# Cross-attention and mixture-of-experts kernel: steps at single places, fewer direct tanh pieces, token lists in 8 by 64

## What is computed

```
x = layernorm(features)                       # 4 x 1024 x 256
h = tanh(txt_proj[:, None] + feat_proj[:, :, None] + b)      # tokens x 77 x 256
rho = einsum('bftd,d->bft', h, w)             # then masked
att = softmax(rho)
w_s, b_s = tanh(att @ text @ Wcw + bcw), tanh(att @ text @ Wcb + bcb)
x = x + (w_s * layernorm(x) + b_s)
...
probs = softmax(layernorm(x) @ gate)
scores, token_idx = top_k(probs.T, k=512)     # for each of 8 experts
out_tok = gelu(tok @ W1 + b1) @ W2 + b2       # times score, added at token_idx
x = x + routed + gelu(x @ Ws1 + bs1) @ Ws2 + bs2
```

## Time and profile before

| | |
|---|---|
| three runs | median 888.53 us (888.24 to 889.59) |
| profiled execution | 887.3 us, of which span 885.5 us |
| TensorE busy | 798.3 us, 90% |
| ScalarE busy | 759.4 us, 86% |
| VectorE busy | 714.6 us, 81% |
| GpSimd busy | 304.9 us, 34% |

### The profile page before, as it was taken

How to read it: one execution, slowest core, us unless ns; L and a number is a source line. 1 busy time by engine, 2 the same in 40 slices (tenths; PEclk the granted TensorE clock), 3 DMA queues, 4 the chain that set the end, 5 groups by cost and what they waited for, 6 DMA issues and landing times.

```text
span 885.5 us, 14111 instructions
## 1 busy us (share of the span) xinstructions
PE 798.3 (90%) x5385; PEld 471.8 (53%) x5385; DVE 714.6 (81%) x1403; ACT 759.4 (86%) x589; POOL 304.9 (34%) x534
## 2 busy tenths in 40 slices
PE   6976678669997999989999899999989999999996
PEld 5321123114442444444454455555766999999886
DVE  5899889898989699997889996895886877666641
ACT  3999999999999999999999999997752676676672
POOL 3200540615443006674002650042404145555424
PEclk9898999899999999999999999999999999999999
DMA  8000000000001000200000010003102365554513
GB/s 260 28 1 0 1 1 1 1 24 1 25 1 48 1 1 25 73 1 1 24 1 1 24 49 1 24 2 119 48 24 84 115 160 143 144 110 123 138 20 41
DMA packets 32406, 41.82 MB, mean 47 GB/s; under 512 B 2365, under 2 KB 29011, under 8 KB 32339
## 3 DMA queue, kind: packets, MB, share of 16 engines
q1 hardware_dynamic: 26083, 32.49, 11.1%
q0 software_dynamic: 6144, 8.39, 5.9%
q10 hardware_dynamic: 112, 0.04, 0.0%
HBM read 28.33 MB, written 12.58 MB: 46 GB/s over the span
## 4 chain that ended last, share of the span: by engine, by line
PE 48%; ACT 24%; DVE 19%; issue 5%; POOL 2%; DMA 1%; POOLq 0%; ACTq 0%; DVEq 0%
ACT z L1001 21%; DVE z L1389 11%; PE bank L920 10%; PE bank L793 10%; PE bank L943 9%; PE bank L850 6%; PE bank L835 5%; PE bank L768 2%; ACT z L997 1%; PE bank L720 1%; DVE att L1460 1%; PE bank L958 1%; ACT u L1050 1%; PE bank L823 1%; POOL xn L1146 1%
## 5 line engine op out<-in xcount | busy, mean ns | idle before, releaser
L1001 ACT ACTIVATE z<-z 128x4096 f32<-128x4096 f32 (+5 forms) x157 | 521.3, 3361 | 7.1 <-DVE z L1389 7.0
L1389 DVE TENSOR_SCALAR z<-feat,txt_bias 128x1024 f32<-128x1024 f32 (+1 forms) x722 | 417.9, 652 | 30.2 <-PE bank L793 29.4
L793 PE MATMUL bank<-z,window 128*32 128x512 f32 x2464 | 301.4, 614 | 61.2 <-ACT z L1001 60.2
L793 PEld LDWEIGHTS bank<-z,window 128*32 128x32 f32 x2464 | 68.1, 111 | 244.3 <-issue 133.2
L850 PE MATMUL bank<-ws_sb,u 128*128 128x256 f32 x512 | 127.2, 389 | 1.4 <-ACT u L1050 1.4
L850 PEld LDWEIGHTS bank<-ws_sb,u 128*128 128x128 f32 x512 | 93.5, 191 | 36.1 <-issue 20.2
L835 PE MATMUL bank<-tr,ws_s 128*128 128x512 f32 x384 | 108.3, 418 | 2.9 <-issue 2.9
L920 PE MATMUL bank<-xg_s,w_s 128*128 128x512 f32 x384 | 99.6, 397 | 0.2 <-DVE xg_s L1712 0.2
L1207 POOL TENSOR_TENSOR scale<-wb,x_ry 128x4 f32<-128x4 f32 x7 | 9.2, 1319 | 253.6 <-ACT wb L1012 253.6
L943 PEld LDWEIGHTS bank<-w_s,hid_s 128*128 128x128 f32 x672 | 86.3, 188 | 4.0
L943 PE MATMUL bank<-w_s,hid_s 128*128 128x256 f32 x672 | 88.2, 280 | 0.0
(11 more groups left out here) (275 smaller groups left out, 777.7 us busy)
## 6 DMA issues: line engine op xcount, KB each, us to landing
w_raw<-in_L_ffn_W_dram SPq DMA_DIRECT2D x16, 1024.0 KB, 5.7
x_ring<-in_x_dram SPq DMA_DIRECT2D x8, 512.0 KB, 7.9
xn_dram<-xn SPq DMA_DIRECT2D x8, 512.0 KB, 2.9
out_dram<-x_ring SPq DMA_DIRECT2D x8, 512.0 KB, 3.2
u<-in_L_ffn_Ws_dram SPq DMA_DIRECT2D x1, 1024.0 KB, 11.8
ws_sb<-in_L_ffn_Ws_dram SPq DMA_DIRECT2D x1, 1024.0 KB, 14.5
xg<-xn_dram,idx POOLq DMA_INDIRECT x32, 4.4
out_dram<-y,idx POOLq DMA_INDIRECT x32, 3.9
```

Source lines behind the costliest of these rows:

```text
L793: ins = e.matmul(sums[v][32 * g:32 * g + 32, :], window[:, c, 31 - at_row:63 - at_row], z[:, n % ZB, at_piece:at_piece + TOK], start=(v, g ...
L1001: e.activation(part, part, ACT.Tanh).then_inc(signal(*step), 1)
L1389: ins = e.tensor_scalar(z[:, n % ZB, i * width:(i + 1) * width], feat_of(units, c), bias_of(units, t, c), None, ALU.add)
```

## The change

- Direct pieces: 64 before, 25 after. The first eight blocks have 7, 5, 0, 4, 1, 3, 1, 1 (before 4, 3, 3, 3, 2, 2, 2, 2); later only blocks 10, 109 and 124 have one (before: 15, 45, 60, 75, 90, 105, 120 and every block that belongs to one unit, 31 to 38 and 129 to 156).
- `PRE`, `TAIL`, `FFN`: places for each unit and slice instead of tables shared by several units and a start with a step.
- Lists: a place (0 to 511) is split into 8 groups of 64 instead of 4 of 128. `pick` is 40 wide (of 64) instead of 20 (of 32), `onehot` 64 instead of 128; the matmul uses two column groups of 64; `listed` writes two halves with a mask `side`.
- Other numbers of filler pieces; `ENDS_BEHIND`, `LAST_END`, `TOGETHER_FROM`.

```diff
-FIRST_DIRECT = (4, 3, 3, 3, 2, 2, 2, 2)
-DIRECT_EVERY = (15, 1)
+FIRST_DIRECT = (7, 5, 0, 4, 1, 3, 1, 1)
+DIRECT = (10, 109, 124)
...
-TAIL_EARLY = (0, 0, 1, 2, 3, 4, 4, 5, 4, 11, 6, 10, 12, 12, 14)
+TAIL = (
+    (2, 3, 4, 6, 5, 7, 8, 9, 10, 20, 10, 13, 14, 15, 22),
...
-FFN = ((8, 2.2), (34, 2.1), (13, 2.3), (36, 2.0), (13, 1.5), (26, 1.6))
+FFN = (
+    (47, 47, 51, 53, 54, 55, 58, 62),
...
-TOGETHER, TOGETHER_FROM = 2, 93
-ENDS_BEHIND = 6
+TOGETHER, TOGETHER_FROM = 2, 91
+ENDS_BEHIND = 3
...
-TAIL_FILL = (7, 3)
-TEST_FILL = (4, 4, 6, 4, 7, 3, 5, 5, 2, 3)
-RANK_FILL = (1, 3, 6, 4)
-EXPERT_FILL = (23, 4, 0)
-SECOND_FILL = (8, 3, 2, 2, 9)
-LIST_FILL = (0, 1, 0, 0)
-LAST_END = 1
+TAIL_FILL = (8, 2)
+TEST_FILL = (5, 5, 4, 5, 7, 4, 3, 6, 4, 4)
+RANK_FILL = (1, 4, 3, 4)
+EXPERT_FILL = (27, 4, 0)
+SECOND_FILL = (8, 4, 0, 2, 11)
+LIST_FILL = (2, 1, 0, 1)
+LAST_END = 0
...
-    if len(units) > 1:
-        return 1 if n % DIRECT_EVERY[0] == 0 and len(pieces) > 2 else 0
-    return 1 if n % DIRECT_EVERY[1] == 0 else 0
+    return 1 if n in DIRECT else 0
...
-                        g = tile % G
-                        ins = e.matmul(dst[32 * g:32 * g + 32, 0:P], pick[:, tile, :], onehot[:, tile, :],
-                                       start=tile < G, stop=tile >= NT - G)
+                        g = tile % 2
+                        ins = e.matmul(dst[LOW * g:LOW * (g + 1), 0:LOW], pick[:, tile, :], onehot[:, tile, :],
+                                       start=tile < 2, stop=tile >= NT - 2)
...
+                    link(e.memset(pick[:, :, V * HIGH:LOW], 0.0))
...
-                    e.tensor_copy(picked[:], banks[LIST][:, 0:P]).then_inc(signal(*step), 1)
+                    for h in range(2):
+                        ins = e.tensor_scalar(picked[:, h * LOW:(h + 1) * LOW], banks[LIST][:, 0:LOW], side[:, h:h + 1], None, ALU.mult)
+                    ins.then_inc(signal(*step), 1)
```

More of the change, by code:

```diff
@@ L161, in work_order @@
         before = starts[bb - 1]
-        at_slots(before, PRE_EARLY, pre(early))
-        at_slots(before, PRE_LATE, pre(late))
+        at_slots(before, PRE[early - 1], pre(early))
+        at_slots(before, PRE[late - 1], pre(late))
         base, early, late = starts[bb], early - UPB, late - UPB
-        at_slots(ends_at[early] + 1, TAIL_EARLY if early else TAIL_FIRST, tail(early))
-        at_slots(base, TAIL_LATE, tail(late))
+        at_slots(ends_at[early] + 1, TAIL[early], tail(early))
+        at_slots(base, TAIL[late], tail(late))
     base = ends_at[va] + 1
[L168 to L172, removed]
+    at_slots(base, TAIL[va], tail(va))
+    for v, places in enumerate(FFN):
+        for m, n in enumerate(places):
             parts = (0, J // 2, J) if v == va - 1 and m == M - 1 else (0, J)
@@ L387, in xattn_moe_kernel @@
     NL = 3
+    HIGH, LOW = 8, 64
     CANDIDATES = (1 << DIGIT) - 1
@@ L390, in xattn_moe_kernel @@
     assert D % P == 0 and CAP == TOK and I <= 32 and NT % JT == 0 and NH == 2 and UNITS % 2 == 0 and P % E == 0
+    assert HIGH * LOW == CAP and HIGH == 2 * A and 2 * LOW == P
     assert T % G == 1 and G == UPB * C and I < 32
@@ L458, in xattn_moe_kernel @@
         V = 5
-        pick = sb("pick", [P, NT, 32], BF16)
         vals = sb("vals", [P, NT, E, V], BF16)
-        iota_slot = gt[:, 0:P]
+        iota_slot = gt[:, 0:LOW]
         bits = tested[:].bitcast(I32).rearrange("p (t e) -> p t e", e=E)
@@ L499, in xattn_moe_kernel @@
         w2_raw = sb("w2_raw", [P, M, D])
-        onehot = sb("onehot", [P, NT, P], BF16)
-        in_tile = sb("in_tile", [P, NT, A], BF16)
+        onehot = sb("onehot", [P, NT, LOW], BF16)
+        pick = sb("pick", [P, NT, LOW], BF16)
+        in_tile = sb("in_tile", [P, NT, HIGH], BF16)
         found = sb("found", [P, V, A])
@@ L1157, in _ @@
             e.memset(b2_raw, 0.0).then_inc(consts, 1)
-            e.memset(pick[:], 0.0).then_inc(consts, 1)
             e.memset(mask_h[0:1], 0.0)
             e.memset(ones_h[0:1, :], 1.0).then_inc(consts, 1)
-            e.iota(iota_slot, [[1, P]], base=0, channel_multiplier=0,
+            e.iota(iota_slot, [[1, LOW]], base=0, channel_multiplier=0,
                    allow_small_or_imprecise_dtypes=True).then_inc(consts, 1)
-            e.iota(iota_a[:], [[1, A]], base=0, channel_multiplier=0,
+            e.iota(iota_a[:], [[1, HIGH]], base=0, channel_multiplier=0,
                    allow_small_or_imprecise_dtypes=True).then_inc(consts, 1)
@@ L1421, in _ @@
                     link(e.tensor_reduce(expert_of[:], ident[:].rearrange("p (t e) -> p e t", e=E), AX.X, ALU.add))
-                    e.tensor_reduce(fold[:], ident[:].rearrange("p (g r) -> p r g", r=32), AX.X, ALU.add)
+                    e.tensor_reduce(fold[:], ident[:].rearrange("p (g q h) -> p q g h", g=2, h=2), AX.XY, ALU.add)
+                    e.tensor_reduce(side[:], ident[:].rearrange("p (q h) -> p h q", h=2), AX.X, ALU.add)
                     e.wait_ge(vector_link, linked)
@@ L1661, in _ @@
                     e.wait_ge(*done("slots"))
[L1662 to L1663 removed]
+                    link(e.tensor_scalar(eq[:].bitcast(I32), slot_i[:], LOW - 1, None, ALU.bitwise_and))
+                    link(e.tensor_scalar(gt[:].bitcast(I32), slot_i[:], LOW.bit_length() - 1, None, ALU.arith_shift_right))
                     e.wait_ge(vector_link, linked)
@@ L1669, in _ @@
                     ex, = args
-                    link(e.tensor_tensor(in_tile[:], slot_a[:, :, ex:ex + 1].broadcast_to([P, NT, A]),
-                                         iota_a[:].unsqueeze(1).broadcast_to([P, NT, A]), ALU.is_equal))
+                    link(e.tensor_tensor(in_tile[:], slot_a[:, :, ex:ex + 1].broadcast_to([P, NT, HIGH]),
+                                         iota_a[:].unsqueeze(1).broadcast_to([P, NT, HIGH]), ALU.is_equal))
                     if ex == 0:
@@ L1676, in _ @@
                     e.wait_ge(vector_link, linked)
-                    e.tensor_tensor(pick[:, :, 0:V * A].rearrange("p t (v a) -> p t v a", v=V),
-                                    in_tile[:].unsqueeze(2).broadcast_to([P, NT, V, A]),
-                                    vals[:, :, ex, :].unsqueeze(3).broadcast_to([P, NT, V, A]),
+                    e.tensor_tensor(pick[:, :, 0:V * HIGH].rearrange("p t (v a) -> p t v a", v=V),
+                                    in_tile[:].unsqueeze(2).broadcast_to([P, NT, V, HIGH]),
+                                    vals[:, :, ex, :].unsqueeze(3).broadcast_to([P, NT, V, HIGH]),
                                     ALU.mult).then_inc(signal(*step), 1)
```

24 lines of the change are left out of this document (12 added, 12 removed), and 18 rows, old and new, of tables (FFN, PRE, TAIL).

## The result

| | before | after |
|---|---|---|
| median of the runs | 888.53 us (5 runs, 886.66 to 890.85) | 882.88 us (5 runs, 878.47 to 885.20) |
| profiled execution: time, span | 887.3, 885.5 us | 882.9, 881.0 us |

The ratio is 0.993 (95% interval 0.991 to 0.995): 0.7% faster. The prediction said 881.0 us, range 875 to 889. Single executions of one kernel lie up to 7 us apart, and most of the low ones have a mean granted TensorE clock near 0.99 instead of 0.98.

A forecast was written before the change was run, and what follows sets the result against it. Bound: ScalarE up to about 400 us, then ScalarE and TensorE both full, then TensorE's fixed list plus idle time. Terms -1.1 + 3.2 + 2.0 + 0 + 3.4 + 0 = 7.5 us less: 881.0 us, range 875 to 889.

The forecast's parts named there:

- likeliest case: Whole kernel: all terms sum to 7.5 us less, 881.0 us, alone 878 to 885; chance 0.50.
- Start: Blocks 0 to 7: first direct piece 1.7 us late, partly offset by fewer waits for adds; net 1.1 us lost.
- Direct pieces in blocks 31 to 38: Tanh stage: eight removed at 0.305 us each; with wide ones elsewhere 3.7 us, taken as 3.2, bounds 0 and 3.7.
- Last 28 blocks: Blocks 129 to 156: one direct piece fewer each, but TensorE takes over as bound; 2.0 us gained.
- New places: Moved steps and FFN slices: same instructions, no TensorE work leaves the full stretch; 0, bounds 4.1 us either way.
- rival "slower": Last 40 blocks: adds shut GpSimd out, normalisation comes late, three stalls of 3.4 us; about 891 us, chance 0.13.
- Search and lists: 606 to 681 us: more filler, shorter lists, less half-clock time; 3.4 us gained, bounds 0 and 7.6.
- filler's: Router search: 47 filler pieces instead of 43 fill TensorE's idle time; 1.6 us gained.
- clock's 0.8: TensorE at half clock in 668 to 674 us: half of 1.5 us missing comes back, 0.8 us gained.
- lists' 1.0: Lists 0 and 1: each 1.2 us shorter, counted as 1.0 us for both; lists 2 to 7 worth nothing.
- List matmuls: 256 list matmuls: half the length but half the groups at once; 0, bounds gain 1 and loss 3.3 us.
- signs of being wrong: ScalarE waiting over 12 us for adds, TensorE waiting for xn, list matmuls above 35 ns, half-clock in the last blocks.

The follow-up runs named there:

- start_old: Changed kernel with the old direct pieces in the first eight blocks and the old places of unit 1's preparation: 881.58 us, ratio 0.9922.
- again: The changed kernel measured once more, nothing altered: 882.42 us, ratio 0.9923 to the kernel before.
- start_tail0: Changed kernel with the edits of start_old and tail0_early together: 878.27 us (4 runs), ratio 0.9889.
- tail0_early: Changed kernel with unit 0's second normalisation placed earlier: 880.95 us, ratio 0.9914.
- singles_direct: Changed kernel with one direct piece back in each of blocks 129 to 156: 884.53 us, ratio 0.9944.
- direct_only: Kernel before with only the direct pieces after the first eight blocks changed as in the change, all places old: 900.33 us (4 runs), ratio 1.0129.
- fills_only: Kernel before with only the new numbers of filler pieces, ENDS_BEHIND and LAST_END: 885.23 us, ratio 0.996.
- lists_only: Kernel before with only the lists in 8 groups of 64: 887.75 us, ratio 0.9992, unresolved by time.
- direct_tail6: direct_only with unit 6's tail steps at their new places: 892.48 us, ratio 1.005.

## Why the prediction was right, and where it was not

The likeliest case held in its total: 7.5 us less forecast, 5.7 and 5.9 measured by the medians of the two comparisons (6.2 and 6.8 by their ratios). Part of that is luck. The places were put at 0 by themselves, which is what they are worth alone; but they decide whether taking the direct pieces out costs 12.0 us or gains 1.5, and the prediction had no term for that. And where the tanh stage gave less than forecast, the search gave more. By its steps:

- **Start (1.1 us lost, bounds 0 and 2.0).** The first direct piece came at 17.20 us, not 17.82: 1.06 late, not 1.7. At block 5 the loss is 3.0, because of the moved preparation, which the step did not count. In time both together are 0.8 by the medians (start_old against again; 0.1 by the ratios) to 2.7 (start_tail0 against tail0_early), neither resolved.
- **Direct pieces in blocks 31 to 38 (part of 3.2).** Right where they stand: 8 x 0.305 = 2.4 forecast, 2.6 from block 30 to 38. But unit 0's normalisation gave 2.7 back between 46 and 50. The prediction had set such a stall at 3.4 us under "places" and then counted none. Taken together, the two terms for direct pieces forecast 5.2 us (3.2 + 2.0); at the new places the removal measured 1.5 (1.9 in the traces).
- **Last 28 blocks (2.0, bounds 0 and 4).** singles_direct measured 2.1 by the medians and 1.3 to 1.8 in the trace, by the mechanism named: TensorE takes over as the bound.
- **New places (0, bounds 4.1 either way).** Here is the step that failed: it priced the places by themselves and added them to the direct pieces. Alone they are 0, as it said. But the removal of the direct pieces is worth +12.0 us at the old places and -1.5 at the new; the two together have an interaction of 13.5 us, over three times the bound. The prediction argued against the rival "slower" with before's steps being on time; but that was their place with 36 adds fewer. In direct_only unit 6's chain came 10.0 us later, was held for 12.34 us, and xn was 3.97 us late for TensorE. The step also took it that no TensorE work leaves the full stretch; one slice's down matmuls (1.99 us) did.
- **Search and lists (3.4).** 4.1 us from the first count on. Fillers gave 3.0 alone, against 1.6 + 0.8 forecast; the lists 1.3 in the trace, against 1.0. In the whole 3.6 + 1.3 would be 4.9. Much of that difference is one thing counted twice: the profiles of both single edits also have a granted clock of 1.00 from the first count to the first expert instead of 0.97, which is worth 0.5 us (54.59 against 54.13, the stretch of the three kernels with 1.00 and neither edit). Set against 54.13, the fillers are worth 3.0 us (fills_only 51.16), with 1.6 forecast, the lists 0.7 (lists_only 53.42), and both together 3.5 (the changed kernel's 50.61). The term that was too small is the filler's; the clock's 0.8 and the lists' 1.0 were a little too large.
- **List matmuls (0, bounds 1 and 3.3).** 0.3 us less busy time in all: right.
- **What was to show it.** "TensorE over 99% in 500 to 606" held (105.07 of 106); "ScalarE below 97%" did not (98.0%); "fewer than 4 us idle before the first expert" held by a hair (1.2 from 606.1 to the first count, 2.77 from there); "last tanh 4 to 6 us earlier" did not (3.0, of which 2 are put-off work). Of the signs of being wrong one came: TensorE waited 6.9 us for GpSimd's xn, 1.9 before.

The rest: the tanh stage was to give 4.1 us (-1.1 + 3.2 + 2.0). In the two profiles it gave 0.4 and -0.7 at the first count, by the medians some 1.6 to 1.8 (5.7 and 5.9 less 4.1). The 2 of unit 0's stall, which tail0_early takes away, and the 2 at block 5 beyond the forecast's 1.1 are about the difference. How much of it the differing clock in the first 60 us adds to a single profile stays open (below).

Of the 12 us of direct_only, 7.9 are shown to be unit 6's late tail. For the other 4.2 there are places in its trace (1.4 to 5.0 us behind from block 30 to 46, where ScalarE waits for adds three times; 5.1 to 10.0 from 128 to 150); they were not taken apart. Whether a direct piece in each block kept before's steps on time by giving VectorE less to do or by leaving pauses in its adds was not tried either.

## What to carry to other kernels

When an edit gives work to an engine that has slack, don't price it by the slack's total: look for the chains of other engines that must run beside that work, and for how long each can be late before its reader stops. An edit of places and an edit of load are one term where the places decide what meets the load; test the pair, since one alone was 12 us slower, the other nothing, and both together 1.7 us faster. And measure progress at a mark behind all work that could have been put off, not at the end of the busiest engine.

## What the hardware showed that I had not expected

**A tiny GpSimd instruction can be held for a whole series of adds.** The first instruction of `y_scale` (four elements a partition) comes after a long wait; in 14 profiles it met 512-wide adds 28 times. 16 times it began 0.15 to 0.29 us after an add's start and took 0.24 to 0.75 us. 12 times it began within 0.08 us of an add's start: one took 0.50, the other eleven 1.65 to 12.34 us, and each of these ended 0.05 to 0.06 us behind the last add of its series (what came next was a pause or another VectorE instruction). The kernel before had two of them (2.08 and 4.50 us). The longer was ended by a pause of 0.03 us between two adds, and its tail could bear it:

```profile
587.90 4.50 POOL L1207 TENSOR_TENSOR scale<-wb,x_ry 128x4 f32<-128x4 f32 x1 [67.42 <-ACT wb L1012]
592.48 0.44 POOL L1209 TENSOR_TENSOR shift<-scale,x_mv 128x4 f32<-128x4 f32 x1
```

So in direct_tail6 two things differ at once: the chain stands 11 us earlier, and it arrived 0.23 us after an add's start, where none was held. Which of the two saved how much was not tried. That the moment of arrival is the cause of the hold is a count, not an experiment. The Trainium skill ("SBUF — State Buffer", Who interferes with whom) says that of a VectorE instruction in a two-port mode and a GpSimd instruction, whichever issues first gets the shared ports for the whole instruction and the other blocks. The traces agree that one blocks: here it was GpSimd, while the adds beside it kept their pace (0.396 us each). In which mode the adds ran no trace shows. That GpSimd can be blocked over 30 instructions in a row (12.34 us) the traces add.

**The first 60 us differ between executions of the same order.** Both direct_only and direct_tail6 have before's order up to there, and their tanh of block 8 ended 2.3 and 0.4 us behind before's. TensorE alone in 20 to 30 and 30 to 40 us (busy, granted clock, DMA share, GB/s), direct_only first:

```profile
20.00:30.00 10.00, 7.57 (x52) 0.83 0.35 115
30.00:40.00 10.00, 8.03 (x45) 0.83 0.00 0
```

```profile
20.00:30.00 10.00, 7.99 (x46) 0.66 0.43 139
30.00:40.00 10.00, 8.91 (x53) 1.00 0.00 0
```

Time at the lower of the clock's two levels, 1.2 GHz, falls at different places: in direct_only there is some between 30 and 40 us too, and behind it VectorE waits 1.53 us for a projection of TensorE (at 41.88 us) and ScalarE 2.95 us for adds (at 52.45), against no such wait and 1.32 in direct_tail6. Seven profiles have before's first eight blocks and unit 1's preparation. Three of them have a granted clock of 1.00 in 30 to 40 us, and their block 8 ends 0.0 to 0.6 us behind before's; the other four have 0.83, and theirs ends 1.8 to 2.4 us behind. So about 2 us at block 8 are no effect of an edit, and the +3.2 of the changed kernel there may be only in part its own. The clock goes with the difference in all seven; it was not varied by itself.
